# Attention scores in eight array tiles, and layer-norm products in four 64x64 tiles, in a fused ViT tower layer on one core

## The chip, the cores and the metric

One core of one Trainium2 chip (trn2) runs the kernel. The metric is the device time of one execution in microseconds, the median of three runs; the profile shown is of one further execution.

## The reference, cut to what matters

Sixteen images of 64 patches are tokenised (two layer norms, projections, SiLU), and the 64 tokens are repeated three times, with a class token ahead: 193 rows of 64 features per image. Then attention with 8 heads of 8 features, whose weights are a softmax plus a relative bias, a layer norm, a residual, another norm, and a routed feed-forward.

```python
h = tok(x)                                   # [16, 192, 64]; three copies of 64 tokens
h = concat([cls_tok, h], axis=1)             # 193 rows
u = layernorm(h)
attn = softmax(q @ k.T * E**-0.5) + rel_bias # 8 heads; q, k, v from u
h = h + layernorm(attn @ v) * gamma + beta
u = layernorm(h)
w = u @ wr + br                              # top 95 of 193 rows of each image are processed
y = gelu(u @ w1 + b1) @ w2 + b2              # 64 -> 256 -> 64
out = where(chosen, y * w, 0) + u + h
```

## The kernel before, in words

Features lie on partitions. Two images form a pair: image 0 of it on partitions 0 to 63, image 1 on 64 to 127, so that eight pairs (`NP`) stand side by side in the free dimension. `bank[0..7]` are the eight PSUM banks, each a tensor of its own. Every engine has one queue of instructions, in the order written, and semaphores between them; there is no planner, so the order is that of the calls: TensorE's (PE) from L1119 on, ScalarE's (ACT) from L399 and L506, VectorE's (DVE) from L739 and L849, GpSimd's (POOL) from L267.

- **Ahead of attention.** `fold` (L1110) sums the bias table's Toeplitz pieces in banks 6 and 7, and `fold_out` (L732) copies them to `rT`, turned by one column so that the class row comes last, in two copies each. `class_sums` (L1029) and `residual_rows` (L1173, one product of 512 columns into bank 2, taken to `hb` at L489) follow later.
- **Attention** goes in four chunks `c` of two pairs. `scores(c)` (L1193) is eight matmuls of 32 rows by 64 columns of weights and 256 columns streamed, into banks 3 and 4 (`SB`): head group g picks the bank, image i the partitions, pair p the half of the bank. Four different places of the array are used, twice. DVE's `softmax_in(c)` (L815) takes the maxima (two reductions, L819), clips them (L821), and subtracts them (L826, two instructions). The next `scores` waits for the last of these. ACT takes the exponential (`exps`, L455), PE turns it (`turn`, L1212, four transposes into bank 6 or 7, `TB[g]`), ACT copies it out to `eT` (`weights_out`, L470), and PE multiplies with the values (`weigh`, L1225). DVE's `normalise(c)` (L829) divides, `softmax_turn(c)` (L1248, four 64x64 matmuls) turns it back and ACT copies it to `pvT` (L485).
- **The bias part**: `table(t, g)` (L1257) is four matmuls of 128 columns, copied out by ACT (`table_out`, L462), added to by POOL (L309) and turned by `table_turn` (L1273). DVE's `add_parts(g)` (L870) sums the parts into `zz`. The class query has a path of its own: `class_query` on PE (L1185) and DVE (L788), `class_query_sums` and `class_query_end`.
- **The two norms.** For each of four groups g of two pairs: `centre` (L1328; 128x128 weights, 386 columns), `squares` on ACT (L545), `variance` (L1338; 128x128 weights with two blocks of ones), `inverse_stds` on ACT (L550: a logarithm L336 and an exponential L339), and on DVE `residual(g)` (L892: L894, L899 twice, L902), which writes `h2`, for the first norm ("z"), `norm(g)` (L906) for the second ("h"). POOL adds `x2` and `h2` to `xh` (L316).
- **Feed-forward.** `route` (L1403) gives the routing weights, on which DVE runs twelve rounds of "eight largest" (L931, L933) and writes `mw` (L936, L938). `up(m)` and `down(m)` (L1369, L1385) are pairs of matmuls in two array tiles; ACT loads the GELU table (L573) and applies it (L586). When the last `down` is done, PE spreads `mw` (L1444), DVE multiplies, DVE and POOL add `xh`, and SP (SyncE) stores.

## Time and profile before

| | us |
|---|---|
| median of three runs (88.22 to 92.36) | 88.4 |
| the profiled execution, its own time | 88.42 |
| its span, first to last instruction | 86.5 |
| PE busy in it | 78.2 |
| DVE busy | 57.5 |
| ACT busy | 55.8 |
| POOL busy | 18.2 |

The rows further down come from the profiled execution. Its own time is 1.92 us above its span. Matmuls are pipelined: the timeline's duration of one reaches to its modelled end, past the start of the next, so that what a step holds PE for is read from the chain of waits, which shows starts and the time to the next. A 4-byte matmul appears as two records ("x2"), a transpose as one.

### The profile page before, as it was taken

How to read it: one execution, taken by the hardware profiler on the slowest of the kernel's cores; microseconds unless marked ns; L12 is line 12 of the kernel's file. 1: busy time of each engine (PE TensorE's matmuls, PEld its weight loads, DVE VectorE, ACT ScalarE, POOL GpSimd, SP SyncE). 2: the span in 40 equal slices, each digit the busy share in tenths (PEclk: the TensorE clock that was granted, in tenths of full speed). 3: DMA queues.
4: the chain of work that ended last, by engine and by line, in shares of the span. 5: the costliest groups of instructions: out<-in, count | busy, mean ns of one | idle time of the engine just before them, and what ended most of it. 6: DMA issues, size and time to landing. Idle time of an engine off the chain costs nothing.

```text
span 86.5 us, 1796 instructions
## 1 busy us (share of the span) xinstructions
PE 78.2 (90%) x638; PEld 49.8 (58%) x638; DVE 57.5 (66%) x188; ACT 55.8 (65%) x122; POOL 18.2 (21%) x31
## 2 busy tenths in 40 slices
PE   3999999999799999999998998999999799999800
PEld 1585758698478457769787865654523242446500
DVE  0299339439465994979989338389925799993860
ACT  0518247788558389885927272799999968995000
POOL 7000000000024553569150000000086300000620
PEclk9999999999999999999999999999999999999995
DMA  1937991000000000000000000000000000000045
GB/s 28 284 139 240 322 361 39 0 0 4 8 0 0 0 11 0 0 0 0 0 8 0 0 0 8 0 0 0 0 0 0 4 0 0 0 0 8 0 152 213
DMA packets 2568, 3.95 MB, mean 46 GB/s; under 512 B 544, under 2 KB 2048, under 8 KB 2560
## 3 DMA queue, kind: packets, MB, share of 16 engines
q1 hardware_dynamic: 1984, 3.31, 12.0%
q10 hardware_dynamic: 576, 0.53, 1.8%
q8 instruction: 5, 0.08, 0.4%
q14 instruction: 3, 0.02, 0.1%
HBM read 3.05 MB, written 0.79 MB: 44 GB/s over the span
## 4 chain that ended last, share of the span: by engine, by line
PE 78%; ACT 8%; DVE 6%; issue 3%; DVEq 1%; POOL 1%; ACTq 0%; POOLq 0%
PE bank L1398 7%; PE bank L1345 6%; PE bank L1335 6%; PE bank L1380 6%; PE bank L1207 5%; PE bank L1268 5%; PE bank L1222 4%; PE bank L1241 4%; PE bank L968 4%; PE bank L960 3%; PE bank L1444 3%; PE bank L1045 3%; PE bank L1253 2%; PE bank L1081 2%; PE bank L1063 2%
## 5 line engine op out<-in xcount | busy, mean ns | idle before, releaser
L586 ACT ACTIVATE gl<-bank,ffw 128x386 f32<-128x386 f32 x16 | 8.1, 583 | 1.0 <-PE bank L1380 1.0
L316 POOL TENSOR_TENSOR xh<-x,h 128x386 f32<-128x386 f32 x4 | 4.0, 1002 | 18.9 <-DVE x L908 18.9
L474 ACT ACTIVATE eT<-bank 128x512 f32<-128x512 f32 x8 | 4.7, 593 | 4.0 <-PE bank L1241 4.0
L1380 PE MATMUL bank<-x,ffw 64*128 64x386 f32 x32 | 6.8, 522 | 0.5 <-ACT gl L586 0.5
L284 POOL TENSOR_SCALAR xTm<-xT,xclsT 128x256 f32<-128x256 f32 x2 | 1.9, 929 | 24.0 <-DVE xT L728 24.0
L1345 PE MATMUL bank<-zq,same 128*128 128x386 f32 x16 | 6.6, 493 | 0.0
L819 DVE TENSOR_REDUCE mx<-bank 128x8 f32<-128x512 f32 x8 | 5.2, 686 | 2.1 <-PE bank L1207 2.0
L309 POOL TENSOR_TENSOR tb<-tb,cterm 128x512 f32<-128x512 f32 (+1 forms) x4 | 5.1, 1270 | 5.4 <-ACT tb L466 5.4
L1398 PE MATMUL bank<-gl,ffw 128*64 128x386 f32 x32 | 6.1, 500 | 0.0
L1241 PEld LDWEIGHTS bank<-vx,eT 128*64 128x64 f32 x128 | 4.3, 137 | 2.0 <-issue 1.2
L826 DVE TENSOR_TENSOR e_in<-bank,mx 128x512 f32<-128x512 f32 x8 | 5.2, 686 | 0.1
L876 DVE TENSOR_TENSOR zz<-bank,pvT 128x192 f32<-128x192 f32 x8 | 2.5, 353 | 4.1 <-ACT pvT L485 2.7
L1241 PE MATMUL bank<-vx,eT 128*64 128x18 f32 x128 | 4.8, 213 | 0.3 <-ACT eT L474 0.3
L346 ACT ACTIVATE pfm<-bank 96x512 f32<-96x512 f32 x4 | 2.4, 589 | 4.3 <-PE bank L968 4.3
L1114 PE MATMUL bank<-toep,idn 128*128 128x193 f32 x24 | 5.1, 335 | 0.0
L1222 PE MATMUL bank<-idn,e 128*128 128x128 f32 x32 | 5.0, 280 | 0.0
L1380 PEld LDWEIGHTS bank<-x,ffw 64*128 64x128 f32 x32 | 2.6, 185 | 4.0 <-issue 3.7
L459 ACT ACTIVATE e<-e_in 128x512 f32<-128x512 f32 x8 | 4.8, 622 | 0.0
L336 ACT ACTIVATE rstd<-bank,eps 128x386 f32<-128x386 f32 x8 | 4.6, 578 | 0.2
L322 POOL TENSOR_TENSOR zq<-zr,xh 128x386 f32<-128x386 f32 x2 | 2.0, 1030 | 12.9 <-DVE zr L944 12.9
L1268 PEld LDWEIGHTS bank<-vx,rT 128*128 128x128 f32 (+1 forms) x32 | 3.8, 164 | 1.3 <-issue 1.1
L1268 PE MATMUL bank<-vx,rT 128*128 128x128 f32 (+1 forms) x32 | 4.4, 280 | 0.0
(187 smaller groups left out, 183.1 us busy)
## 6 DMA issues: line engine op xcount, KB each, us to landing
out<-zq SPq DMA_DIRECT2D x4, 193.0 KB, 2.1
toep<-toeplitz SPq DMA_DIRECT2D x1, 642.0 KB, 4.1
vx<-vx_start SPq DMA_DIRECT2D x1, 576.0 KB, 6.0
ptm<-patches_tm ACTq DMA_DIRECT2D x2, 192.0 KB, 3.4
ptm<-patches_tm SPq DMA_DIRECT2D x2, 192.0 KB, 3.5
atw<-attw SPq DMA_DIRECT2D x1, 352.0 KB, 2.8
ffw<-ffnw SPq DMA_DIRECT2D x1, 321.0 KB, 6.4
cst<-const SPq DMA_DIRECT2D x1, 131.0 KB, 4.8
```

What stands on the lines that cost most here:

```text
L309: pool.tensor_tensor(tb[0:rows_t, t, 8 * g:8 * g + 8, :], tb[0:rows_t, t, 8 * g:8 * g + 8, :], bc(cterm[0:rows_t, t].rearrange("p h d -> p ...
L586: act.activation(gl[:, 2 * (m % SLOTS) + t, :], bank[UB[m % 2][t]][:, 0:GC], ACT.Gelu_apprx_tanh, bias=b1[:, m % 2:m % 2 + 1]).then_inc(s[ ...
L819: dve.tensor_reduce(mx0[:, c, g, :], sc[g], AX, ALU.max).then_inc(s["mx0_ready"], 1)
L826: dve.tensor_tensor(e_in[:, g], sc[g], bc(mx[:, c, g, :], 2, J), ALU.subtract)\
L1114: last = pe.matmul(bank[6 + b // 2][:, S * (b % 2):S * (b % 2) + S], ident, toep[:, b, J * c:J * c + S], start=(c == 0), stop=(c == 2))
L1222: last = pe.transpose(bank[TB[g]][:, 128 * b:128 * b + 128], e[:, g, 128 * b:128 * b + 128], ident)
L1241: last = pe.matmul(bank[PVB[c]][r, 72 * j + 18 * b:72 * j + 18 * b + 18], eT[:, g, 2 * j + hh, r], vx[:, 2 * c + j, b, 2 * i:2 * i + 2, :] ...
L1268: last = pe.matmul(out_v[:, :, :, b, :].rearrange("q a t c -> q (a t) c"), rT[:, b, 128 * t:128 * t + rows_t], vx[:, 4 * g:4 * g + 4, b, : ...
L1335: pe.matmul(bank[CB[g]][:, 0:GC], cent, src, start=True, stop=True)\
L1345: pe.matmul(bank[RB[g]][:, 0:GC], same_image, zq[:, g, :], start=True, stop=True)\
L1380: last = pe.matmul(bank[UB[m % 2][t]][:, 0:GC], view(ffw, FFNW, "ffn_w1")[r, 128 * c:128 * c + 128], x2[r, g, :], start=True, stop=True)
L1398: last = pe.matmul(bank[FB[g]][64 * t:64 * t + 64, 0:GC], view(ffw, FFNW, "ffn_w2")[:, 64 * c:64 * c + 64], gl[:, 2 * (m % SLOTS) + t, :], ...
```

## The change

Each part, in the order of the kernel:

- The eight PSUM banks become one tensor of eight banks, and banks are dealt anew. `SB` is now a bank for each head group and image (banks 2, 3, 6, 7), and `scores` puts the pair j on the partitions: its eight matmuls stand on eight different places of the array. DVE reads two banks in one instruction. The halves of `eT`, `mx`, `weigh` change index accordingly.
- All turned attention weights go through one bank (`TB = 4`), apart from the last, which uses bank 7; a `turn` waits for the copy-out of the turn before.
- `softmax_turn` is one 128x128 transpose; `table` is two matmuls of 256 columns instead of four of 128.
- `centre` is two 64x64 matmuls, from rows r to the other half of the output partitions; `variance` is two 64x64 matmuls from rows r to the same half. So each `centre` swaps the two images of a pair. `residual_rows` is done in the same swapped way in two halves, earlier, into bank 7. The second `centre` swaps back. Since `xh` needs `h2` unswapped, SP issues eight transfers from `h2` into a new tile `h2_own`, and POOL's additions wait for all eight.
- The class row is first instead of last, so `rT` is copied in one instruction for two, `wts` and `mw` are written by one instruction each, and the host no longer reorders the output.
- The order of calls on PE, ACT and DVE changes around all of these.

```diff
-BT = (5, 3, 4, 2)
-CB = (5, 3, 4, 2)
-RB = (6, 7, 1, 0)
+BT = (5, 3, 6, 2)
+CB = (5, 3, 6, 2)
+RB = (4, 7, 1, 0)
...
-WB = 6
-FB = (4, 0, 2, 6)
+WB = 4
+FB = (6, 0, 2, 4)
...
-KB, QB, VB = (6, 6), (2, 5), (7, 0)
+KB, QB, VB = (4, 4), (2, 5), (1, 0)
...
-SB, TB = (3, 4), (6, 7)
+SB, TB = ((2, 3), (6, 7)), 4
...
+            for g in range(G):
+                sp.wait_ge(s["h2_ready"], 3 * g + 3)
+                for t in range(2):
+                    r, r_other = slice(64 * t, 64 * t + 64), slice(64 - 64 * t, 128 - 64 * t)
+                    sp.dma_start(h2_own[r, g, :], h2[r_other, g].rearrange("p a q -> p (a q)"))\
+                        .then_inc(s["h2_own_ready"], 16)
...
             for g in range(G):
                 pool.wait_ge(s["x2_ready"], g + 1)
-                pool.tensor_tensor(xh[:, g, :], x2[:, g, :], h2[:, g].rearrange("p a q -> p (a q)"),
-                                   ALU.add).then_inc(s["xh_ready"], 1)
+                pool.wait_ge(s["h2_own_ready"], 32 * G)
+                pool.tensor_tensor(xh[:, g, :], x2[:, g, :], h2_own[:, g, :], ALU.add).then_inc(s["xh_ready"], 1)
...
             square4(1)
+            residual_rows_out()
             keys(0)
             head_keys(0, (2, 3))
             std4(1)
             values_out(0)
-            residual_rows_out()
+            keys(1)
+            queries()
+            values_out(1)
             class_key_exp(0)
-            keys(1)
-            values_out(1)
-            queries()
             exps(0, 0)
             exps(0, 1)
+            values_rows_out()
             head_keys(1, (2, 3))
...
             squares("z", 0)
-            softmax_part_out(2)
             squares("z", 1)
+            squares("z", 2)
             softmax_part_out(3)
             inverse_stds("z", 0)
-            squares("z", 2)
             inverse_stds("z", 1)
...
-                dve.tensor_copy(rT[:, 2 * i:2 * i + 2, 0:S - 1], src[:, :, 1:S]).then_inc(s["rT_ready"], 1)
-                dve.tensor_copy(rT[:, 2 * i:2 * i + 2, S - 1:S], src[:, :, 0:1]).then_inc(s["rT_ready"], 1)
+                dve.tensor_copy(rT[:, 2 * i:2 * i + 2, :], src).then_inc(s["rT_ready"], 1)
...
             def softmax_in(c):
-                sc = [bank[SB[g]][:, :].rearrange("p (h k) -> p h k", k=J) for g in range(2)]
+                sc = [banks[:, SB[g][0]:SB[g][0] + 2, 0:256].rearrange("p i (h k) -> p i h k", k=J)
+                      for g in range(2)]
...
             class_query()
             softmax_in(2)
+            normalise(0)
             class_query_sums()
-            normalise(0)
             softmax_in(3)
             normalise(1)
+            normalise(2)
             class_query_end()
...
             add_parts(0)
             add_parts(1)
-            normalise(2)
+            add_parts(2)
             normalise(3)
-            add_parts(2)
             add_parts(3)
...
             def scores(c):
...
-                for p in (2 * c, 2 * c + 1):
+                for j in range(2):
                     for i in range(2):
                         for g in range(2):
                             r = slice(64 * i + 32 * g, 64 * i + 32 * g + 32)
-                            last = pe.matmul(bank[SB[g]][64 * i:64 * i + 64, 256 * (p % 2):256 * (p % 2) + 256],
-                                             qT[r, p, :], k_h[r, p].rearrange("p h k -> p (h k)"),
+                            last = pe.matmul(bank[SB[g][i]][64 * j:64 * j + 64, 0:256], qT[r, 2 * c + j, :],
+                                             k_h[r, 2 * c + j].rearrange("p h k -> p (h k)"),
                                              start=True, stop=True)
...
             def turn(c, g):
                 pe.wait_ge(s["e_ready"], 2 * c + g + 1)
-                if c:
-                    pe.wait_ge(s["eT_ready"], 2 * c + g - 1)
-                elif g == 0:
+                t = bank[TB]
+                if (c, g) == (0, 0):
                     pe.wait_ge(s["kT_ready"], 2)
+                elif (c, g) == (NC - 1, 1):
+                    t = bank[SB[1][1]]
+                    pe.wait_ge(s["ein_ready"], 2 * NC)
                 else:
-                    pe.wait_ge(s["vx_ready"], 1)
-                    pe.wait_ge(s["vx2_ready"], 1)
+                    pe.wait_ge(s["eT_ready"], 2 * c + g)
...
             def softmax_turn(c):
                 pe.wait_ge(s["o_ready"], c + 1)
-                for j in range(2):
-                    for i in range(2):
-                        r = slice(64 * i, 64 * i + 64)
-                        last = pe.matmul(bank[PVB[c]][r, 256 + J * j:256 + J * j + J], o[r, c, J * j:J * j + J],
-                                         ident[r, r], start=True, stop=True)
-                last.then_inc(s["pvT_psum"], 1)
+                pe.transpose(bank[PVB[c]][:, 256:384], o[:, c, :], ident).then_inc(s["pvT_psum"], 1)
...
             scores(0)
-            residual_rows()
             keys(1)
+            queries(1)
             values(1)
-            queries(1)
             values_rows()
             scores(1)
-            table(*TABLE[0])
             turn(0, 0)
             class_query()
+            table(*TABLE[0])
+            turn(0, 1)
+            weigh(0, 0)
+            scores(2)
+            turn(1, 0)
             table(*TABLE[1])
-            turn(0, 1)
-            scores(2)
+            weigh(0, 1)
+            weigh(1, 0)
+            turn(1, 1)
             table(*TABLE[2])
-            turn(1, 0)
-            weigh(0, 0)
-            weigh(0, 1)
-            turn(1, 1)
-            table(*TABLE[3])
             scores(3)
-            weigh(1, 0)
             softmax_turn(0)
             turn(2, 0)
-            table_turn(0)
+            table(*TABLE[3])
             weigh(1, 1)
             turn(2, 1)
             weigh(2, 0)
+            softmax_turn(1)
+            weigh(2, 1)
+            table_turn(0)
             table_turn(1)
             turn(3, 0)
+            softmax_turn(2)
+            turn(3, 1)
             table_turn(2)
-            softmax_turn(1)
-            turn(3, 1)
-            weigh(2, 1)
+            weigh(3, 0)
...
-                pe.matmul(bank[CB[g]][:, 0:GC], cent, src, start=True, stop=True)\
-                    .then_inc(s["zc_psum" if name == "z" else "hc_psum"], 1)
+                for t in range(2):
+                    r, r_other = slice(64 * t, 64 * t + 64), slice(64 - 64 * t, 128 - 64 * t)
+                    last = pe.matmul(bank[CB[g]][r_other, 0:GC], cent[r, r], src[r, :], start=True, stop=True)
+                last.then_inc(s["zc_psum" if name == "z" else "hc_psum"], 1)
...
-                pe.matmul(bank[RB[g]][:, 0:GC], same_image, zq[:, g, :], start=True, stop=True)\
-                    .then_inc(s["zvar_psum" if name == "z" else "hvar_psum"], 1)
+                for t in range(2):
+                    r = slice(64 * t, 64 * t + 64)
+                    last = pe.matmul(bank[RB[g]][r, 0:GC], same[r, r], zq[r, g, :], start=True, stop=True)
+                last.then_inc(s["zvar_psum" if name == "z" else "hvar_psum"], 1)
 
             centre("z", 0)
-            weigh(3, 0)
             weigh(3, 1)
-            softmax_turn(2)
             centre("z", 1)
+            centre("z", 2)
             variance("z", 0)
             softmax_turn(3)
             table_turn(3)
-            centre("z", 2)
             variance("z", 1)
...
             route(0)
             variance("h", 3)
+            up(0)
             route(1)
-            up(0)
             route(2)
...
             down(2)
+            up(6)
             down(3)
-            up(6)
             up(7)
```

## Rows read from the trace of the kernel before

**Rows 1.** The page, busy time by engine: busy us (share), records.

```profile
PE 78.2 (90%) x638; PEld 49.8 (58%) x638; DVE 57.5 (66%) x188; ACT 55.8 (65%) x122; POOL 18.2 (21%) x31
```

**Rows 2.** Table of stretches: length, then busy us of each engine, granted clock, DMA share, GB/s.

```profile
33.60:50.10 16.50, 16.24 (x226) 13.29 (x222) 13.64 (x32) 10.95 (x25) 6.34 (x5) 1.00 0.00 1
...
55.05:66.17 11.12, 11.12 (x42) 5.08 (x40) 7.65 (x22) 10.60 (x23) 2.59 (x3) 1.00 0.00 0
66.17:79.05 12.88, 12.31 (x70) 4.71 (x70) 10.97 (x41) 10.93 (x20) 1.42 (x2) 1.00 0.01 2
```

**Rows 3.** The chain of waits, attention and norms: start, us, engine, tile, line.

```profile
24.70 0.85 PE bank L1036 x8
...
28.00 1.02 PE bank L1207 x16
29.02 1.05 PE bank L1176 x2
...
34.72 0.44 PE bank L1222 x4
...
38.35 1.09 PE bank L1268 x8
...
43.98 0.38 PE bank L1253 x8
...
45.97 0.61 ACT eT L474
...
46.71 0.65 PE bank L1241 x16
...
57.33 0.65 PE bank L1345 x2
```

**Rows 4.** Timeline of DVE, attention stage; in brackets the idle time before it.

```profile
33.70 1.29 DVE L819 TENSOR_REDUCE mx<-bank 128x8 f32<-128x512 f32 x2 [1.33 <-PE bank L1207]
...
35.23 1.29 DVE L826 TENSOR_TENSOR e_in<-bank,mx 128x512 f32<-128x512 f32 x2
...
36.44 0.68 DVE L791 TENSOR_REDUCE cq_m<-bank 128x8 f32<-128x512 f32 x1
...
38.42 1.29 DVE L819 TENSOR_REDUCE mx<-bank 128x8 f32<-128x512 f32 x2 [0.37 <-PE bank L1207]
...
43.47 1.29 DVE L819 TENSOR_REDUCE mx<-bank 128x8 f32<-128x512 f32 x2 [0.26 <-PE bank L1207]
...
51.08 0.62 DVE L876 TENSOR_TENSOR zz<-bank,pvT 128x192 f32<-128x192 f32 x2 [2.48 <-ACT pvT L485]
```

**Rows 5.** Timeline of ACT and DVE in the two norms.

```profile
55.05 0.58 ACT L336 ACTIVATE rstd<-bank,eps 128x386 f32<-128x386 f32 x1
...
60.71 0.62 DVE L894 SCALAR_TENSOR_TENSOR zr<-bank,tkw,rstd 128x386 f32<-128x386 f32 x1
...
60.95 0.58 ACT L336 ACTIVATE rstd<-bank,eps 128x386 f32<-128x386 f32 x1
...
61.91 0.16 DVE L902 TENSOR_TENSOR h<-zr,hb 128x2 f32<-128x2 f32 x1
...
62.37 0.57 ACT L336 ACTIVATE rstd<-bank,eps 128x386 f32<-128x386 f32 x1
```

**Rows 6.** The chain of waits, feed-forward.

```profile
71.88 0.80 PE bank L1398 x4
...
76.48 2.74 PE bank L1398 x16
```

**Rows 7.** DMA issues: KB each, median us from issue to landing.

```profile
out<-zq SPq DMA_DIRECT2D x4, 193.0 KB, 2.1
```

**Rows 8.** Timeline, first and last of the feed-forward: ACT's table, DVE's last routing row.

```profile
66.17 1.28 ACT L573 ACT_TABLE_LOAD   x1
...
78.48 0.15 DVE L938 SCALAR_TENSOR_TENSOR mw<-cur,wts 128x1 f32<-128x1 f32 x1
```

More of the change, by code:

```diff
@@ L94, in sem @@
             return ctx.enter_context(nc.semaphore(name))
-        bank = [ctx.enter_context(nc.psum_tensor(f"bank{i}", [128, 512], F32)) for i in range(8)]
+        banks = ctx.enter_context(nc.psum_tensor("bank", [128, 8, 512], F32))
+        bank = [banks[:, i, :] for i in range(8)]
         ptm = sb("ptm", 128, NT, PF)
@@ L465, in table_out @@
                 act.wait_ge(s["tb_psum"], n + 1)
-                act.activation(tb[0:rows_t, t, 8 * g:8 * g + 8, :],
-                               bank[5][0:rows_t, :].rearrange("p (a f) -> p a f", a=8), ACT.Copy)\
+                act.activation(tb[0:rows_t, t, :, 32 * g:32 * g + 32],
+                               bank[5][0:rows_t, :].rearrange("p (a f) -> p a f", a=B), ACT.Copy)\
                     .then_inc(s["tb0_ready"], 1)
@@ L473, in weights_out @@
                     act.wait_ge(s["pv_psum"], c)
-                act.activation(eT[:, g].rearrange("p a n -> p (a n)"), bank[TB[g]][:, :], ACT.Copy)\
+                t = bank[SB[1][1] if (c, g) == (NC - 1, 1) else TB]
+                act.activation(eT[:, g].rearrange("p a n -> p (a n)"), t[:, :], ACT.Copy)\
                     .then_inc(s["eT_ready"], 1)
@@ L492, in residual_rows_out @@
                 act.wait_ge(s["hbias_ready"], 1)
-                act.activation(hb[:, :, 0:J], bank[2][:, :].rearrange("p (a j) -> p a j", a=NP), ACT.Identity,
+                act.activation(hb[:, :, 0:J], bank[7][:, :].rearrange("p (a j) -> p a j", a=NP), ACT.Identity,
                                bias=hbias[:, :]).then_inc(s["hb_ready"], 1)
@@ L497, in values_rows_out @@
                 act.wait_ge(s["vt_psum"], 1)
-                act.activation(vT[:, :, :], bank[2][:, :].rearrange("p (a j) -> p a j", a=NP), ACT.Copy)\
+                act.activation(vT[:, :, :], bank[1][:, :].rearrange("p (a j) -> p a j", a=NP), ACT.Copy)\
                     .then_inc(s["vT_ready"], 1)
@@ L1027, in class_projections, with class_sums @@
                           view(atw, ATTW, "wv")[0:64, :], start=True, stop=True).then_inc(s["cls_psum"], 1)
-            def class_sums(t):
+            def class_sums(t, bs):
                 n = (128, J + 1)[t]
                 pe.wait_ge(s["cls_qkv"], 3)
-                pe.wait_ge(s["rT_ready"], 4)
+                pe.wait_ge(s["rT_ready"], 2 if 0 in bs else 1)
                 pe.wait_ge(s["in_const"], 16)
-                for b in range(4):
+                for b in bs:
                     last = pe.matmul(bank[1][0:n, 32 + 8 * t + 2 * b:34 + 8 * t + 2 * b], rT[:, b, 128 * t:128 * t + n],
@@ L1108, in queries, with residual_rows @@
                     .then_inc(s["q_psum"], 1)
+            def residual_rows(a):
+                pe.wait_ge(s["h1_ready"], a + 1)
+                pe.wait_ge(s["rT_ready"], 1)
+                for t in range(2):
+                    r, r_other = slice(64 * t, 64 * t + 64), slice(64 - 64 * t, 128 - 64 * t)
+                    last = pe.matmul(bank[7][r_other, 256 * a:256 * a + 256], view(atw, ATTW, "wp2_bd")[r, r],
+                                     h1T[r, 256 * a:256 * a + 256], start=True, stop=True)
+                if a:
+                    last.then_inc(s["hf_psum"], 1)
             def fold(b, cs):
@@ L1152, in _ @@
             fold(1, (0, 1))
+            fold(1, (2,))
             project3(0)
-            fold(1, (2,))
+            class_sums(0, (2, 3))
+            residual_rows(0)
             variance4(0)
+            class_sums(0, (0, 1))
             project3(1)
-            class_sums(0)
+            residual_rows(1)
             keys(0)
-            queries(0)
+            class_sums(1, range(4))
             variance4(1)
@@ L1188, in class_query @@
                 pe.wait_ge(s["kT_ready"], 2)
-                pe.wait_ge(s["vT_ready"], 1)
-                pe.matmul(bank[2][:, :], qcls_m[:, :], kT[:, :], start=True, stop=True)\
+                pe.wait_ge(s["vx_ready"], 2)
+                pe.wait_ge(s["vx2_ready"], 2)
+                pe.matmul(bank[0][:, :], qcls_m[:, :], kT[:, :], start=True, stop=True)\
                     .then_inc(s["cq_psum"], 1)
@@ L1235, in weigh @@
                 pe.wait_ge(s["eT_ready"], 2 * c + g + 1)
-                for j in range(2):
+                for i in range(2):
                     for hh in range(2):
-                        for i in range(2):
-                            r = slice(64 * i, 64 * i + 64)
+                        for j in range(2):
+                            r = slice(64 * j, 64 * j + 64)
                             b = 2 * g + hh
-                            last = pe.matmul(bank[PVB[c]][r, 72 * j + 18 * b:72 * j + 18 * b + 18],
-                                             eT[:, g, 2 * j + hh, r],
+                            last = pe.matmul(bank[PVB[c]][r, 72 * i + 18 * b:72 * i + 18 * b + 18],
+                                             eT[:, g, 2 * i + hh, r],
                                              vx[:, 2 * c + j, b, 2 * i:2 * i + 2, :].rearrange("p t d -> p (t d)"),
@@ L1496, in _lay_out @@
     tc = np.zeros((2, 128, H), np.float32)
-    tc[0] = table[S:S + 128]
-    tc[1, 0:J] = table[S + 128:S + 3 * J]
-    tc[1, J] = table[S - 1]
+    tc[0] = table[S - 1:S + 127]
+    tc[1, 0:J + 1] = table[S + 127:S + 3 * J]
     vx0 = np.zeros((2, 64, NP, 4, 2, 2, D + 1), np.float32)
```

132 lines of the change are left out of this document (64 added, 68 removed).

## The prediction

> **What bounds the kernel now.** I began with busy time by engine: PE is busy for 78.2 of 86.5 us, DVE and ACT for under 58 each [rows 1]. Taken alone this says that PE is the bound and that four array tiles instead of one should pay. The table of stretches says otherwise [rows 2]. In attention (33.6 to 50.1) PE is busy for 16.24 of 16.50 us, but DVE for 13.64 too; in the norms (55.05 to 66.17) PE for all 11.12 and ACT for 10.60. So I read the chain for what each step holds PE for [rows 3], the timeline of DVE for what it waits for [rows 4], and the norms' timeline for a period [rows 5].
>
> In attention there is a loop: `scores(c+1)` waits until DVE has subtracted chunk c, and DVE then waits for `scores(c+1)`. DVE's idle ahead of chunks 1, 2 and 3 is 1.33, 0.37 and 0.26 us, and later it waits 2.48 us for `pvT` of chunk 1 ahead of the second group's sum, because PE turns that chunk late [rows 4]. In the norms everything has one period: logarithm to logarithm on ACT 62.37 - 60.95 = 1.42 us, and DVE's residual from 60.71 to 61.91 + 0.16 = 62.07, 1.36 and a start each 1.4 [rows 5]. PE needs 2 x 0.65 = 1.3 for a centre and a variance [rows 3]. Three engines are tied; relieving PE alone shortens nothing here.
>
> **The parts and their costs.** The sum goes against the profiled execution, 88.42 us, 0.02 above the median, with 1.92 outside the span.
>
> *Ahead of the first scores.* `class_sums` (0.85 for one set of four [rows 3]) and the class column's copies move into idle places; `project3(1)`, the first keys and ACT's logarithm for the second half keep their inputs. The first scores still need the query copy, which DVE now does last. I take 0 for the start at 28.0 and keep -0.1 to +0.4, the upper end being half a `class_sums` that falls on the path.
>
> *Scores.* Before: eight matmuls on four places, two rounds, 1.02 [rows 3]. A round is 256 columns; one `variance` of 386 columns takes 0.65 [rows 3], so a round is 256/386 x 0.65 = 0.43, and 1.02 = 2 x 0.43 + 0.16 for entering the mode. With eight places one round is left: 0.43 + 0.16 = 0.6, unless sixteen records can't be issued so fast; `weigh` issues sixteen in 0.55 to 0.65 [rows 3], so 0.6 stands. Gain 0.4 for each of three chunks on the path. Bounds: 0 (no overlap in one row strip) and 0.5.
> The row that bears on this is `down`: its two matmuls use all 128 rows and different columns, and sixteen records, eight matmuls, take 2.74, 0.34 each, half of 0.65 [rows 3, 6]. So neighbours in one row strip do overlap.
> The Trainium skill, "TensorE: Matmul & The Clock Gate", Part 3, "The mechanism", says that a weight load overlaps running matmuls only when its row group differs; by that the new scores and norm tiles would gain nothing (the second rival). The trace's `down` disagrees with it.
>
> *The schedule of attention.* I redid it with the rows' durations: PE to DVE 0.15 us, PE to ACT 0.3, ACT to PE 0.13 (46.58 to 46.71 [rows 3]); ACT's 512-element operations 0.55 to 0.6; `softmax_in` 2 x 1.29 + 0.2 = 2.8 (33.70 to 36.44 [rows 4]); the class query on DVE 1.6. `residual_rows` (1.05 [rows 3]) no longer stands between the first scores and the second keys, and `table(0)` (1.09) no longer between scores and turn.
> Chunk 0 leaves DVE at 31.75, scores(1) is issued at once instead of behind `values_rows`, and DVE starts chunk 1 at 32.5 instead of 33.70. It ends it at 35.25, does the class query to 36.85 and finds scores(2) (issued 35.8, done 36.5) ready: chunk 2 at 36.85 instead of 38.42, to 39.65. Then normalise(0) and the class sums, 1.75, to 41.4; scores(3) is ready by 40.9; chunk 3 at 41.4 instead of 43.47, to 44.2. So 2.1 us are gained there, and DVE is the bound: behind chunk 3 come normalise(1), a wait of 1.0 for `weigh(2, 1)`, normalise(2), the end of the class query and three sums, to 49.75. PE centres group 0 at 48.55, then weighs the last half chunk, centres groups 1 and 2, and multiplies variance 0 beside centre 2, done at 51.3. The 2.48 us wait is gone; late instead is ACT's queue, which holds the squares of groups 0 to 2 and the last `pvT`: its first logarithm is at 52.2 instead of 55.05 [rows 5]. Gain 2.85.
> `softmax_turn` falls from 0.38 to the 0.11 of one transpose (four take 0.44 [rows 3]), `table` from 1.09 by the three starts saved to some 0.9; both are inside this schedule.
> An unknown is DVE's reading over two banks. The shortest rows of one bank cost 1.29/2 for 512 elements, 1.26 ns each; the cut-up sums of L876 0.31 for 192, 1.61 ns each [rows 4]. At the latter rate each of sixteen instructions costs 0.18 more, 2.9 together. I take 0, as the new pattern still runs 64 elements in a row and the cut into heads is there already.
>
> *The norms.* Centre and variance now lie side by side, 0.65 to 0.8 a pair for 1.3. ACT doesn't get shorter: eight logarithm-exponential pairs and the squares, 11.12 us from 55.05 [rows 2, 5]. One square (group 2), 0.4, is now done ahead, so from 52.2 it lasts 10.7, to 62.9 instead of 66.17. That is 3.25 gained, all but 0.4 of it from attention. The tiles' own share here is nothing: PE gets idle. What they would be worth on top is bounded by 0 and by 8 x 0.65 = 5.2, and the ACT row puts it at the low end; without it the swap of halves would not be needed.
>
> *The transfers* stand on SP's queue, which holds only the output's behind them. A transfer of 193 KB takes 2.1 us [rows 7]; those of 99 KB for the last group start near 59 and land near 62. POOL's four additions (1 us each) end by 67 at the latest. Nobody needs `xh` until `mw` is ready, 78.6 [rows 8]. Cost 0; without that cover a late one would cost its 2 us once.
>
> *Feed-forward.* It hangs on ACT's last exponential (the table load starts at 66.17 [rows 8], and GELU after it) and on the routing that follows the last `x2`. DVE's routing becomes shorter by two single-column instructions, 0.15 and 0.2, but PE is later than `mw`: its `down` block, 76.48 + 2.74, ends after 78.63 [rows 6, 8]. The new order splits down 2, down 3, up 6, up 7 into four blocks for two. A `down` alone takes 0.80, in a block 2.74/4 = 0.69 [rows 6]: 0.11 a block, with `up` somewhat more, so I take +0.3 (0 to +0.4).
>
> Sum: 88.42 - 3.25 + 0.3 = 85.5. A hand-made schedule has each instruction start the moment that its input is there. For what slips (a copy-out behind another, seven turns through one bank) I add 0.4, an estimate from the idle times of 0.26 and 0.37 that the present kernel shows in a like place [rows 4]. **Forecast 85.9 us.**
>
> **Rivals.**
> 1. *The turning bank becomes the bound* (slower). With one bank for seven of eight turns, a turn can't start until ACT has copied the last one out: 0.3 + 0.61 + 0.13 = 1.04 us [rows 3], and this copy stands in ACT's queue behind exponentials, head keys and table copies. In my schedule scores, tables and `weigh` cover it, but it already makes the second turn of chunk 0 one to two us later than its exponential. For it: ACT is busy for 10.95 of 16.5 in attention [rows 2] and its order is fixed. Against it: DVE is the busier one. Each round trip that isn't covered costs 1.04; from the third on, 85.9 + 2.5 is reached and the change is a loss. With four, 90.1; I price it at 89.8.
> 2. *No overlap within a row strip.* Scores stay at 1.02, 3 x 0.4 = 1.2 back, and the norm's pairs at 1.3 plus entering the mode, about 0.4: 87.5. Against it: `down`.
> 3. *DVE pays for two banks*: 85.9 + 2.9 = 88.8, as DVE is the bound.
> 4. *PE's clock falls.* The granted clock is 1.00 in all the stretches [rows 2], with PE never short of work. In the norms it would now be busy for about half of the time. If the level falls from 2.4 to 1.2 GHz there, a side-by-side pair takes 1.3, still inside ACT's 1.42, but the first blocks of the feed-forward would run at half speed: four of them at 0.8 more each, about 89. The Trainium skill, the page named above, Part 1, says that activity releases the throttle; no run here shows what half a load does.
> 5. *Better than scheduled*: no slip, and no cost of the split blocks: 84.8.
>
> **How the numbers follow.** Forecast 0.50 (its own range 85.2 to 87.0); rival 1 0.12, rival 2 0.12, rival 3 0.08, rival 4 0.06, rival 5 0.12. The range 84.6 to 88.8 leaves out about 0.05 below and 0.12 above. Two per cent, about what a measurement of this kernel can tell from no change, is 1.77 us. Under 86.6: 0.44 of the forecast, rival 5, and 0.05 of rivals 2 and 3, 0.61. Over 90.2: half of rival 1 and of rival 4, 0.10 with what isn't named. Between: 0.29.
>
> **What would show it.** Right: a `scores` step of about 0.6 in the chain, DVE's first maxima of chunks 1 to 3 near 32.5, 36.9 and 41.4, the wait of 2.48 gone, ACT's first norm logarithm near 52.2 and a period of 1.42 from there, the table load near 62.9, PE idle by a third or more in the norms, and from there to the end the same length or 0.3 more. Wrong: idle DVE in attention with PE waiting for `eT`; a reduction over 0.7 us; a granted clock under 1 behind the norms; a period in the norms well under 1.42, which would mean that ACT wasn't bound; POOL's additions reaching past the end of the routing.

## The result, and the profile after

The kernel after takes 86.26 us (median of four runs, 86.0 to 90.86) against 88.32 us (median of four, 88.22 to 92.36) for the kernel before beside it. The ratio is 0.9761, 95% interval 0.9728 to 0.9794: 2.1 us less (1.8 to 2.4). Forecast were 85.9 us, with a range of 84.6 to 88.8. The profiled execution took 86.00 us, its span is 84.2.

One thing must be known before any two traces are laid side by side: the first products of an execution run at half rate for a time that differs from execution to execution, with the same code. The first `variance2` product started at 12.2 us in this trace, at 13.0 in the trace before, and between 12.4 and 15.8 in those below, most of which leave the code ahead of it alone. Executions that were over 1.5% slower than the fastest of their kernel, as those that began late are, stay out of the ratios. I read every trace from that product on, in four stretches, each ending at an instruction's start: the first `scores` (start), the first logarithm of the norms (attention), the GELU table load (norms), the end of DVE's last addition (feed-forward).

| stretch, us | before | after | measured | forecast |
|---|---|---|---|---|
| start: first `variance2` to first `scores` | 14.97 | 15.32 | +0.35 | 0 |
| attention: to the first logarithm | 27.12 | 25.26 | -1.86 | -2.85 |
| norms: to the table load | 11.12 | 10.46 | -0.66 | -0.4 |
| feed-forward: to DVE's last addition | 17.42 | 17.88 | +0.46 | +0.3 |
| slips | | | | +0.4 |
| sum | 70.63 | 68.92 | -1.71 | -2.55 |

The profiled executions differ by 88.42 - 86.00 = 2.42: the 1.71, plus 0.74 from the earlier first product, less 0.03 behind DVE's last addition. The 0.74 lies within what one and the same code shows from execution to execution, so I don't count it as the change's. The nearly right total thus hides a gain that was forecast 0.8 us too high.

Busy time by engine, kernel after (answers to [rows 1]):

```profile
PE 72.9 (87%) x632; PEld 43.9 (52%) x632; DVE 57.7 (69%) x184; ACT 55.6 (66%) x122; POOL 18.1 (21%) x31
```

PE lost 5.3 us of work and the kernel 2 us: the other engines' work is as it was.

Table of stretches, kernel after: attention, norms, feed-forward to the spreading of `mw` (columns as in [rows 2]):

```profile
32.50:50.00 17.50, 15.80 (x211) 11.58 (x209) 15.56 (x40) 11.96 (x28) 6.25 (x5) 1.00 0.00 1
...
52.80:63.26 10.46, 8.82 (x65) 2.71 (x64) 7.46 (x22) 10.16 (x23) 1.02 (x2) 1.00 0.32 76
63.26:76.63 13.37, 12.29 (x68) 4.41 (x66) 10.79 (x39) 10.81 (x20) 2.86 (x3) 1.00 0.01 2
```

In attention DVE, busy for 15.56 of 17.50, has all but caught up with PE, 15.80. In the norms PE idles for 1.6 us, ACT hardly at all, and the clock stays at 1.00.

The chain of waits, kernel after (start, us, what; answers to [rows 3] and [rows 6]):

```profile
31.44 0.62 PE bank L1227 x16
...
37.45 0.60 PE bank L1263 x16
...
38.13 0.61 ACT eT L483
...
38.88 0.65 PE bank L1263 x16
...
43.19 0.60 PE bank L1263 x16
...
43.87 0.61 ACT eT L483
...
44.61 0.63 PE bank L1243 x4
...
70.62 0.80 PE bank L1416 x4
71.42 0.07 issue
71.49 0.92 PE bank L1398 x4
72.41 0.80 PE bank L1416 x4
73.21 0.85 PE bank L1398 x4
```

`scores` (L1227) holds PE for 0.62 instead of 1.02. At two places PE runs dry for 0.83, from 38.05 to 38.88 and from 43.79 to 44.61: ACT's copy to `eT` (L483) begins only when a `weigh` (L1263) has ended, because `eT` has one buffer and `weights_out(c, g)` waits until all of chunk c-1 is weighed. The kernel before has the same wait in its code, and its chain shows it once for 0.83, with the rows 45.97 and 46.71 of [rows 3]. New is the one at 38.05, which lies ahead of `scores(3)`.

DVE's timeline, attention stage, kernel after (answers to [rows 4]):

```profile
32.16 1.29 DVE L828 TENSOR_REDUCE mx<-bank 128x8 f32<-128x512 f32 x2 [0.40 <-PE bank L1227]
33.48 0.17 DVE L830 TENSOR_SCALAR mx<-mx 128x16 f32<-128x16 f32 x1
...
36.43 1.28 DVE L828 TENSOR_REDUCE mx<-bank 128x8 f32<-128x512 f32 x2
...
40.56 0.71 DVE L811 SCALAR_TENSOR_TENSOR cq_den<-cq_c,cq_s 128x8 f32<-128x8 f32 x1
...
41.73 1.29 DVE L828 TENSOR_REDUCE mx<-bank 128x8 f32<-128x512 f32 x2 [0.23 <-PE bank L1227]
43.06 0.60 DVE L830 TENSOR_SCALAR mx<-mx 128x16 f32<-128x16 f32 x1
...
46.70 0.17 DVE L844 SCALAR_TENSOR_TENSOR den<-ec,bank 128x16 f32<-128x16 f32 x1 [1.02 <-PE bank L1263]
```

POOL's timeline, the same stretch:

```profile
39.90 1.26 POOL L317 TENSOR_TENSOR tb<-tb,cterm 65x512 f32<-65x512 f32 x1 [2.47 <-ACT tb L474]
41.13 1.28 POOL L314 TENSOR_TENSOR cq_v<-cq_e,vT 128x512 f32<-128x512 f32 x1
42.37 1.26 POOL L317 TENSOR_TENSOR tb<-tb,cterm 128x512 f32<-128x512 f32 x1
```

The wait of 2.48 is gone, and two reductions, each over two banks, cost 1.29, as over one. But two tiny operations are stretched: the clip of the maxima (L830) takes 0.17 or 0.60, and `cq_den`, 128x8 elements, 0.71. Both long ones end within 0.11 us of the end of a POOL operation (39.90 + 1.26 = 41.16, 42.37 + 1.26 = 43.63). The Trainium skill, "SBUF — State Buffer", "Who interferes with whom", gives the reason: VectorE and GpSimd share one pair of SBUF ports as an exclusive lock, which an operation with two SBUF inputs or in a two-port mode needs and `tensor_reduce` never does. By that rule, the trace agrees: the large reductions beside the same POOL operations keep their 0.64, and so do subtractions, which have one input in PSUM (1.29 for two from 40.22 in the trace before, beside a POOL operation from 40.15).

ACT's timeline, kernel after (answers to [rows 5]):

```profile
52.80 0.59 ACT L344 ACTIVATE rstd<-bank,eps 128x386 f32<-128x386 f32 x1
...
56.80 0.58 ACT L344 ACTIVATE rstd<-bank,eps 128x386 f32<-128x386 f32 x1
...
58.21 0.58 ACT L344 ACTIVATE rstd<-bank,eps 128x386 f32<-128x386 f32 x1
...
63.26 1.28 ACT L582 ACT_TABLE_LOAD   x1
```

The period is 58.21 - 56.80 = 1.41, as before.

### The profile page after: what moved, and what is told of

The parts are those of the page before. It is cut to its first block, busy times and chain, and to the rows that moved or that the text cites. A ratio compares the mean times of both kernels' runs of the same rounds, so it can differ in the third digit from the quotient of the medians.

```text
span 84.2 us, 1799 instructions
## 1 busy us (share of the span) xinstructions
PE 72.9 (87%) x632; PEld 43.9 (52%) x632; DVE 57.7 (69%) x184; ACT 55.6 (66%) x122; POOL 18.1 (21%) x31
## 4 chain that ended last, share of the span: by engine, by line
PE 72%; ACT 16%; DVE 4%; issue 3%; DVEq 1%; POOL 1%; ACTq 0%; POOLq 0%
PE bank L1416 7%; PE bank L1398 6%; PE bank L1263 6%; PE bank L1131 5%; PE bank L1243 5%; PE bank L1285 4%; ACT rstd L347 4%; ACT rstd L344 3%; PE bank L974 3%; PE bank L1353 3%; PE bank L966 3%; PE bank L1462 3%; ACT zq L557 3%; PE bank L1227 2%; PE bank L1051 2%
## 5 line engine op out<-in xcount | busy, mean ns | idle before, releaser
L325 POOL TENSOR_TENSOR xh<-x,h_own 128x386 f32<-128x386 f32 x4 | 3.9, 1003 | 16.0 <-DMA h_own<-h 16.0
L483 ACT ACTIVATE eT<-bank 128x512 f32<-128x512 f32 x8 | 4.7, 592 | 3.9 <-PE bank L1263 3.1
L1365 PE MATMUL bank<-zq,same 64*64 64x386 f32 x32 | 6.9, 508 | 0.1
L1263 PE MATMUL bank<-vx,eT 128*64 128x18 f32 x128 | 5.2, 213 | 0.8 <-ACT eT L483 0.8
L1263 PEld LDWEIGHTS bank<-vx,eT 128*64 128x64 f32 x128 | 4.4, 137 | 2.9 <-issue 2.6
L557 ACT ACTIVATE zq<-bank 128x386 f32<-128x386 f32 x8 | 3.9, 483 | 2.1 <-PE bank L1353 2.1
L1353 PE MATMUL bank<-h,cst 64*64 64x386 f32 x16 | 3.5, 510 | 1.5 <-DVE h L912 1.3
L330 POOL TENSOR_TENSOR zq<-zr,xh 128x386 f32<-128x386 f32 x2 | 2.0, 1012 | 12.2 <-DVE zr L950 12.2
L1243 PEld LDWEIGHTS bank<-idn,e 128*128 128x128 f32 x32 | 3.5, 141 | 1.8 <-issue 1.3
```

Source lines behind the costliest of these rows:

```text
L557: act.activation(zq[:, g, :], bank[CB[g]][:, 0:GC], ACT.Square)\
L1243: last = pe.transpose(t[:, 128 * b:128 * b + 128], e[:, g, 128 * b:128 * b + 128], ident)
L1263: last = pe.matmul(bank[PVB[c]][r, 72 * i + 18 * b:72 * i + 18 * b + 18], eT[:, g, 2 * i + hh, r], vx[:, 2 * c + j, b, 2 * i:2 * i + 2, :] ...
L1353: last = pe.matmul(bank[CB[g]][r_other, 0:GC], cent[r, r], src[r, :], start=True, stop=True)
L1365: last = pe.matmul(bank[RB[g]][r, 0:GC], same[r, r], zq[r, g, :], start=True, stop=True)
```

## The experiments

Four groups, each on one chip beside runs of the kernel before. All are edits of the kernel after. Stretches as above, in us; the ratio is to the kernel before.

| run | start | attention | norms | feed-forward | sum | ratio, 95% |
|---|---|---|---|---|---|---|
| before | 14.97 | 27.12 | 11.12 | 17.42 | 70.63 | 1 |
| after | 15.32 | 25.26 | 10.46 | 17.88 | 68.92 | 0.9761 [0.9728, 0.9794] |
| c0_changed | 15.32 | 25.27 | 10.45 | 17.90 | 68.94 | 0.9808 [0.9715, 0.99] |
| e1_ff_order | 15.32 | 25.27 | 10.45 | 17.41 | 68.45 | 0.9787 [0.9724, 0.985] |
| e2_full_norms | 15.10 | 25.74 | 10.92 | 17.90 | 69.66 | 0.99 [0.981, 0.9989] |
| e3_two_eT | 16.63 | 28.52 | 10.44 | 17.90 | 73.49 | 1.0204 [1.0153, 1.0254] |
| e4_two_eT_order | 15.31 | 29.44 | 10.45 | 17.89 | 73.09 | none |
| e5_third_round | 15.32 | 28.51 | 10.45 | 17.89 | 72.17 | 1.0176 [1.009, 1.0262] |
| e6_all | 15.31 | 29.24 | 10.45 | 17.41 | 72.41 | 1.0263 [1.0203, 1.0323] |
| e7_residual_later | 15.72 | 25.26 | 10.46 | 17.91 | 69.35 | 0.9871 [0.9812, 0.993] |
| e8_no_shared_port | 15.31 | 25.37 | 10.45 | 17.88 | 69.01 | 0.9837 [0.9796, 0.9878] |
| e9_all_no_shared_port | 15.32 | 23.35 | 10.45 | 17.39 | 66.51 | 0.9514 [0.9487, 0.9542] |
| e10_dry_spell_filled | 15.31 | 24.98 | 10.45 | 17.39 | 68.13 | 0.9697 [0.964, 0.9754] |
| e11_best_third_round | 15.31 | 24.82 | 10.46 | 17.40 | 67.99 | 0.9728 [0.9687, 0.977] |

The stretches repeat to 0.03 us in every run that doesn't touch them (e3's start apart), so they tell apart what a ratio can't, whose interval reaches 0.25 to 0.8 us to either side. By their ratios alone most of these runs can't be told from the kernel after; what they price is read from the stretches of one trace each.

**c0_changed.** The kernel after, unedited.

> The changed kernel itself, as the measure for the others of this group: 86.2 us by every theory, first norm logarithm at 52.8 and table load near 63.3 in its trace. A second profile also tells how much of the 0.39 us by which its first scores started earlier than before (27.54 against 27.93) comes back: if the lead stays it is a part of the gain, if it goes it was the arrival of the input.

Every stretch came back; the first `variance2` product stood at 14.74 instead of 12.22, which is 2.5 of the 2.8 us by which this execution, at 88.81, was longer. The chain of waits of c0_changed, early:

```profile
7.84 1.05 PE bank L1051 x4
...
9.84 1.05 PE bank L1051 x4
10.89 0.85 PE bank L1062 x8
```

The same three steps take 0.58, 0.58 and 0.44 in the trace of the kernel after.

**e1_ff_order.** The calls of the feed-forward in the old order.

```diff
+            down(3)
             up(6)
-            down(3)
```

> The feed-forward's old order of blocks (down 2, down 3, up 6, up 7). Theory: splitting them costs two changes of array mode, so 0.3 to 0.5 us come back, about 85.8, and the stretch from the table load to the spreading of mw goes from 13.5 back to 13.1. Rival: the routing on DVE or ACT's GELU bounds that stretch, then no change, 86.2.

0.49 us came back. Chain of waits of e1_ff_order at the same place:

```profile
70.15 0.85 PE bank L1398 x4
71.00 1.45 PE bank L1416 x8
72.45 1.50 PE bank L1398 x8
```

Two `down` in one block take 1.45 against 2 x 0.80, two `up` 1.50 against 0.92 + 0.85, and 0.07 of waiting goes: 0.15 + 0.27 + 0.07 = 0.49. The break between kinds of tile costs more where it ends at an `up`.

**e2_full_norms.** Centres, variances and residual rows as 128x128 products again, with no swap and no transfers.

```diff
-                for t in range(2):
...
-                    last = pe.matmul(bank[CB[g]][r_other, 0:GC], cent[r, r], src[r, :], start=True, stop=True)
...
+                pe.matmul(bank[CB[g]][:, 0:GC], cent, src, start=True, stop=True)\
...
-                    last = pe.matmul(bank[RB[g]][r, 0:GC], same[r, r], zq[r, g, :], start=True, stop=True)
...
+                pe.matmul(bank[RB[g]][:, 0:GC], same_image, zq[:, g, :], start=True, stop=True)\
...
```

> Centres and variances as 128x128 products again, residual rows unswapped, no transfers of h2; all else as changed. Theory: ACT bounds the norms with its period of 1.41 us, so PE's 64x64 tiles buy nothing by themselves: 86.2, within 0.3, the period of the logarithms still 1.41 to 1.44. Rival: side-by-side tiles carry a good part of the gain: 87.0 or more, with PE as the releaser of ACT's squares and a period of 1.5 or over. A second rival, that the eight transfers cost something by sharing memory with the engines: faster, under 86.0.

The tiles are worth 0.48 ahead of the first logarithm and 0.46 behind it, and their residual rows cost 0.22 at the start: 0.72 net. ACT's timeline of e2_full_norms shows where:

```profile
57.55 0.58 ACT L338 ACTIVATE rstd<-bank,eps 128x386 f32<-128x386 f32 x1 [0.16 <-PE bank L1353]
...
58.97 0.57 ACT L338 ACTIVATE rstd<-bank,eps 128x386 f32<-128x386 f32 x1
```

In the middle the period is 58.97 - 57.55 = 1.42, so ACT is the bound with either kind of tile. The tiles pay at the joints. Ahead of the first logarithm PE makes two centres and a variance, side by side in 1.46 us (50.77 to 52.23 in the chain of the kernel after) and one behind the other in 2.14 here (50.81 to 52.95). Behind it, of the seven intervals from logarithm to logarithm, the second, the third and the last are 0.14, 0.15 and 0.17 longer here; at the passage from the first norm to the second (57.55) and at the end (63.03) ACT waits for a variance. The transfers cost nothing behind the table load, where the stretches with and without them are equal (17.88 and 17.90); in the norms this run takes away the transfers and the tiles together and can't tell them apart. So the theory, no change, and the rival's period of 1.5 were both wrong.

**e3_two_eT.** A second buffer of `eT`, so that a copy-out waits for the chunk before the last.

```diff
...
-                if c:
-                    act.wait_ge(s["pv_psum"], c)
+                if c > 1:
+                    act.wait_ge(s["pv_psum"], c - 1)
...
-                                             eT[:, g, 2 * i + hh, r],
+                                             eT[:, c % 2, g, 2 * i + hh, r],
```

> A second buffer for the turned weights eT, so that a copy-out no longer waits for the last chunk's products; PE's two waits of 0.83 us (38.05 and 43.79 in the changed kernel's trace) go. Theory: DVE is the bound in attention and gets back only its 0.23 us ahead of chunk 3; from the first scores to the first norm logarithm 25.26 falls to about 25.0, 86.0 in all. Rival: PE's waits were on the path, 2 x 0.83: 23.6, about 84.6.

The waits for `eT` went, and the kernel became 2% slower than the one before. The start stretch was 1.3 longer in this execution, and the half rate accounts for it, not the edit (e4, e6 and e9 have the same buffers and 15.3): here it reached past the first `variance2`, and the first five steps of PE's chain from there took 3.30 us against 2.02 in the kernel after. Attention took 3.3 more, and the granted clock was 0.50 from 51 to 57 us. What lowered it shows better in e6.

**e4_two_eT_order**, the same with `weigh(2, 1)` ahead of `softmax_turn(1)`, and **e6_all**, e4 with e1's order and ACT's `exps(3, 0)` ahead of `softmax_part_out(1)`.

```diff
+            weigh(2, 1)
             softmax_turn(1)
-            weigh(2, 1)
```

> As e3_two_eT, and PE weighs the second half of chunk 2 ahead of softmax_turn(1) instead of behind it, so that DVE's normalise(2) needn't wait the 1.02 us. Theory (DVE bound): 1.0 less than e3_two_eT from first scores to first norm logarithm, about 24.1, 85.0 in all. Rival: ACT's queue (exponentials of chunk 3 behind the copy of pvT) is next and holds it at 24.7 or more.

> As e4_two_eT_order, with the feed-forward's old order of blocks, and ACT taking the first exponential of chunk 3 ahead of the copy of pvT. By the theories: 0.49 less than e4_two_eT_order behind the table load (13.37 to 12.88, which e1_ff_order showed), and 0.2 to 0.4 less ahead of the norms: 84.3. If ACT isn't next, only the 0.49: 84.5.

Both came out far above that. Table of stretches of e6_all:

```profile
44.00:48.00 4.00, 2.45 (x38) 2.24 (x39) 3.79 (x11) 1.94 (x5) 0.78 (x1) 0.74 0.00 0
48.00:51.00 3.00, 3.00 (x17) 2.91 (x16) 1.55 (x8) 1.35 (x4) 0.00 (x0) 0.50 0.00 0
...
54.00:57.00 3.00, 3.00 (x26) 1.52 (x25) 0.71 (x3) 0.78 (x3) 0.00 (x0) 0.64 0.00 0
```

The granted clock falls from 2.4 to 1.2 GHz near 46 us, inside a stretch in which PE was busy for 2.45 of 4.00, and stays there for most of the time to 56. PE had just idled from 44.54 to 45.59, waiting for `eT`. In e4 five of six executions had a mean clock of 0.93 and took 90.44 us or more; the sixth, of the same code, had 0.987 and took 86.36, which leaves no ratio. Why PE ran dry stands in DVE's timeline of e6_all:

```profile
41.24 1.59 DVE L811 SCALAR_TENSOR_TENSOR cq_den<-cq_c,cq_s 128x8 f32<-128x8 f32 x1
...
44.25 0.55 DVE L830 TENSOR_SCALAR mx<-mx 128x16 f32<-128x16 f32 x1
```

and in POOL's:

```profile
40.31 1.27 POOL L314 TENSOR_TENSOR cq_v<-cq_e,vT 128x512 f32<-128x512 f32 x1
41.55 1.26 POOL L317 TENSOR_TENSOR tb<-tb,cterm 128x512 f32<-128x512 f32 x1
```

With PE no longer held, the table reaches POOL 1.5 us earlier, counted from the first `scores`, and `cq_den` meets another pair of its operations: it is held through the rest of one and all of the next, until 41.55 + 1.26 = 42.81. In the kernel after POOL's operations follow each other as closely, and there `cq_den` got its turn between two of them, at 41.16; what decides which it will be no run shows. Chunk 3 leaves DVE late. ACT's queue has the exponential of its maxima ahead of the copy of `eT` for chunk 2, so that ACT idles for 1.40 us, and PE, which needs the copy, for 1.05.

**e5_third_round.** `scores` issues its first four products twice (the result is the same), so that the step costs PE what it did before.

```diff
-                for j in range(2):
+                for j in (0, 0, 1):
```

> Each chunk of scores issues its first four products twice, so that a chunk takes two rounds on PE as before the change (about 1.05 us instead of 0.62). Theory: the one-round scores gain their 0.43 us on each chunk that DVE waits for, and DVE waits for chunks 1 and 3 (idle 0.40 and 0.23) but is late itself at chunk 2: 0.43 + 0.43 lost of 1.3, about 87.1. Rival: PE's order decides everything there, then all three count, 87.5 or more. Rival: DVE has slack enough, then 86.3.

The step went from 0.62 to 1.02, and attention from 25.26 to 28.51. Four rounds of 0.4 are 1.6; the rest I put down to the clock, which fell again. Table of stretches of e5_third_round:

```profile
48.00:51.30 3.30, 2.45 (x46) 2.03 (x44) 1.78 (x7) 2.61 (x7) 1.26 (x1) 1.00 0.00 0
51.30:54.80 3.50, 3.50 (x24) 3.27 (x24) 2.57 (x11) 1.84 (x4) 0.00 (x0) 0.52 0.02 5
```

So this run can't price the round; e11 was made for that. Its PE waits twice for 0.85 us, hardly more than the twice 0.83 of the kernel after, whose clock held: what decides whether it falls stays open.

**e7_residual_later.** `residual_rows(0)` behind `variance4(0)`.

```diff
+            variance4(0)
             residual_rows(0)
-            variance4(0)
```

> residual_rows(0), the 64x64 products ahead of variance4(0), moved behind it. Theory: they cost 0.22 us before the first scores (from variance2(0) to the first scores 15.32 us, 15.10 with 128x128 products in e2_full_norms, 14.97 before the change); 15.1 here and 86.05 in all. Rival: not their place but the later queries set it: 15.3, 86.26.

It got worse by 0.40 at the start, against both theory and rival: PE now idles for 0.32 ahead of `variance4(0)`, where these products used to be, and the second half's next product, `project3(1)`, starts 0.55 later. So of the 0.35 lost at the start, 0.22 is known from e2 as the price of doing these rows in tiles; the other 0.13 stays open.

**e8_no_shared_port.** `cq_den` and the two clips become reductions, which don't need POOL's ports. ACT writes `exp(-m)/3` as a 65th column of `cq_e`, and the maxima get a column of zeros beside them.

```diff
...
-                dve.scalar_tensor_tensor(cq_den[:, :], cq_c[:, :], 1.0 / 3.0, cq_s[:, :], ALU.mult, ALU.add)\
...
+                dve.tensor_reduce(cq_den[:, :], cq_e[:, :, :], AX, ALU.add).then_inc(s["cq_den_ready"], 1)
...
-                    dve.tensor_scalar(mx[:, c], mx0[:, c], 0.0, None, ALU.max)
+                    dve.tensor_reduce(mx[:, c], mx0[:, c], AX, ALU.max)
```

> The changed kernel with DVE's small operations on the softmax replaced: the class denominator's addition (0.71 us in the changed kernel's trace, 0.17 where POOL is idle) is folded into a reduction over one more column that ACT writes, and the clipping of the maxima (0.60 us once, else 0.17) is a reduction over the value and a zero. Theory: these two waited for POOL's running additions, and reductions don't; both go. Chunk 3 is also held by PE (scores(3) issued at 40.94), so of 0.97 us only the 0.43 of the clipping reach the norms: from first scores to first norm logarithm 24.85, about 85.85. Rival: the length is the instructions' own, and a reduction over POOL's running time is as long: no change, 86.26. Second rival: PE then waits longer for its input and its clock falls as in e3_two_eT: 88 or more.

No gain. DVE's timeline of e8_no_shared_port:

```profile
43.03 0.20 DVE L819 RECIPROCAL cq_r<-cq_den 128x8 f32<-128x8 f32 x1
44.27 1.29 DVE L833 TENSOR_REDUCE mx<-bank 128x8 f32<-128x512 f32 x2 [1.04 <-PE bank L1233]
```

DVE is free earlier and then idles for 1.04 until the scores of chunk 3 come, which stand behind PE's wait for `eT`; what the clip gives back goes into a longer wait for `weigh(2, 1)`, 1.44 for 1.02. The two holds lie side by side: to take this one away alone gives nothing.

**e9_all_no_shared_port.** e6 and e8 together.

> e6_all with the same replacement. Theory: in e6_all the class denominator's addition took 1.59 us behind two operations of POOL, so that chunk 3 began 2.4 us after its scores were issued; PE ran dry from 44.4 and its clock fell to half until 56. With the addition gone chunk 3 begins 1.5 us earlier; if the clock holds, from first scores to first norm logarithm about 22.5 us and 83.0 in all. Rival: PE, which has less to do than DVE here, runs dry all the same and the clock falls: 88 or more, logarithm over 27.

DVE's timeline of e9_all_no_shared_port at the same place:

```profile
42.54 0.68 DVE L817 TENSOR_REDUCE cq_den<-cq_e 128x8 f32<-128x520 f32 x1
43.26 0.20 DVE L819 RECIPROCAL cq_r<-cq_den 128x8 f32<-128x8 f32 x1
43.38 1.25 DVE L833 TENSOR_REDUCE mx<-bank 128x8 f32<-128x512 f32 x2
44.66 0.19 DVE L836 TENSOR_REDUCE mx<-mx 128x16 f32<-128x32 f32 x1
```

Nothing is stretched, DVE waits for nothing here, and the clock is 1.00 in every stretch from 44 to 60. Attention takes 23.35, 1.91 less than after the change, though 0.85 more than I expected. When DVE begins to subtract chunk 3 the lead is 1.47, and that much is the two holds', as the calls that e4 and e6 moved come later; the rest, with the wait for `weigh(2, 1)` down from 1.02 to 0.48, may be the new order's, and no run separates it. In the chain of e9_all_no_shared_port a copy through the one turning bank now shows, for which PE waits 0.68:

```profile
45.99 0.60 ACT eT L488
...
46.65 0.65 PE bank L1269 x16
```

At 0.9514, with 83.8 us in the shortest of seven executions (median 86.19), it beats both kernels.

**e10_dry_spell_filled.** e6 with five products of 512 bf16 columns, written where nobody reads, in the place in which PE ran dry (the edit is shown against e6; the trace has a record of four of the five).

```diff
+            pe.wait_ge(s["tb0_ready"], 4)
+            keep_busy(5, 5)
             weigh(2, 1)
```

> e6_all with five idle products (128x128 bfloat16 weights, 512 columns, into a bank that nobody reads) where PE ran dry at 44.4; nothing else. They leave the arithmetic as it is. Theory: the clock fell because PE had too little to do there; with the products it stays at full level, and from first scores to first norm logarithm 29.24 falls to about 24.9 (e9_all_no_shared_port's 23.35 and the 1.6 us by which POOL holds DVE ahead of chunk 3), 85.3 in all. Rival: the fall has another cause, then the length stays over 28, 90.2.

PE's timeline, and below it the table of stretches, of e10_dry_spell_filled:

```profile
43.64 0.65 PE L1263 MATMUL bank<-vx,eT 128*64 128x18 f32 x16
44.44 1.03 PE L966 MATMUL bank<-warm 128*128 128x512 bf16 x4 [0.16 <-issue]
```

```profile
44.00:48.00 4.00, 3.28 (x44) 2.53 (x44) 3.72 (x11) 2.13 (x5) 0.51 (x1) 1.00 0.00 0
```

The clock is 1.00 in the stretches behind, too. One microsecond of products that nobody needs gives back 29.24 - 24.98 = 4.26 us, as expected. That the dry spell brings the clock down in e6 is thereby shown. The run also shows what the second `eT` buffer gives with the clock held and `cq_den` still at 1.59: 0.28, new order included.

**e11_best_third_round.** e9 with e5's edit.

> e9_all_no_shared_port with each chunk's first four scores products issued twice, so that a chunk takes two rounds, as before the change. It measures the price of the second round where the clock has held (in e5_third_round it fell). Theory: DVE waits for chunks 0 and 1 only and starts chunks 2 and 3 straight from other work, so 0.3 + 0.42 are lost: 23.35 from first scores to first norm logarithm becomes 23.9 to 24.1 (the scores' own start is the same), about 84.6. Rival: all four count, 1.7: 25.0, 85.6. Second rival: the clock falls: over 26.

The clock held, and attention took 24.82 - 23.35 = 1.47 more: most of 4 x 0.4. My schedule had put three steps on the path, with DVE's slack behind one of them; nearly all four count (the rival's 25.0 was the better forecast).

## Why the prediction was right, and where it wasn't

- **Scores: right.** A step of 0.6 was forecast, 0.62 came. Eight places run side by side although they share row strips, as `down` had said; the second rival falls. The rule quoted beside it is about weight loads, and these overlapped too: in the `down` block before, from 76.48 to 79.22, the loads (PEld) of the same 128 rows, all but the first four, lie inside the time of its products. The stage's gain from the shorter step is larger than three steps of 0.4, 1.47 measured on e9; on the kernel after itself it has no price, as the clock fell in e5.
- **Reading over two banks: right.** 0.64 a reduction, as before; the third rival falls.
- **Start: wrong by 0.35**, inside its bound of +0.4: "I take 0" should have counted the residual rows, which moved ahead of the second keys, as two tiles more, 0.22 (e2).
- **The schedule of attention: wrong by 1.0**, with 0.4 set aside for it, and by 1.5 with norm products of 128x128 (e2: 25.74 against 24.27). The failed steps are two. "scores(3) is ready by 40.9": I took `weigh` to be ready when its exponential was and left out that `eT` has one buffer, so that PE waits 0.83 ahead of `scores(3)` and once more behind it, though [rows 3] shows such a wait. And "normalise(0) and the class sums, 1.75": these were costed at undisturbed durations, where POOL adds 0.5 to `cq_den`. The trace before had the sign: its clip at 39.74 takes 0.45, beside a POOL operation from 38.89 to 40.16. Measured from the first `variance2`, chunk 1 was 0.4 later than scheduled, chunk 2 0.3, and chunk 3 1.1.
- **Tiles in the norms: wrong.** "The tiles' own share here is nothing" was read from a period, and the period is indeed ACT's. But a stage has joints too, where ACT waits for a product, and two centres and a variance lie ahead of the period altogether. Gross 0.94, net 0.72 (e2), which is over a third of the change's 1.71. In attention 0.48 of it hides half a microsecond of the schedule's error. Two signs named for "right" failed with it: a pair side by side takes 0.97 (53.70 to 54.67), not 0.65 to 0.8, and PE idles for 1.64 of 10.46 in the norms, not for a third. The square done ahead, forecast at 0.4, gave 0.20 (11.12 before, 10.92 in e2); the tiles made up for it.
- **Transfers: right.** `xh` was written from 62.2 to 66.1, 12 us ahead of its use.
- **Feed-forward: sign right, size low**, +0.49 (e1) for +0.3: 0.15 of it at the `down`, 0.27 at the `up`, 0.07 of waiting. The prediction had 0.11 a block, from a quarter of a block of four; a block of two, 1.45, stood in the trace before.
- **First rival, the turning bank:** round trips were uncovered, but by another cause. There are two, of 0.83 instead of 1.04, one more than before; I had put the loss at the third. Their cause is the single `eT`, not the bank: e9 keeps the one bank, and neither of the two is left in its chain. The bank itself shows there once, with 0.68.
- **Fourth rival, the clock:** it stayed at 1.00 in attention, norms and feed-forward. But e3 to e6 show it one step away, and not in the norms, where I looked for it, but in attention. I had put its price at about 3 us; it was 4.26 in e6.

Adding up what was priced: scores -1.5 and norm tiles -0.9, against +0.35 at the start and +0.49 in the feed-forward, give -1.6 of -1.71. So the new order of calls in attention and the cheaper `table` and `softmax_turn` seem to leave next to nothing: what they free goes into the two holds, without which attention is 1.5 to 1.9 shorter (e9). This balance mixes prices from two versions and is argued, not measured as a whole.

## What to carry to other kernels

Before an engine's queue is scheduled by hand, write down each buffer's number of copies and each pair of engines that hold one another, since two holds side by side can hide each other until both are removed. Don't price a stage by its period alone: its first and last turns follow other engines than its middle. And when a faster order leaves TensorE dry, look at the granted clock first: here dummy products were worth four times their time.

## What the runs showed of the hardware

- An operation of DVE on 128x8 elements took 0.17 (before), 0.71 (after) or 1.59 us (e6) by where POOL stood. Between two POOL operations that followed each other it got its turn in the kernel after and didn't in e6.
- TensorE's level fell to 1.2 GHz after PE had idled for 1.05 us (e6), in a stretch busy for 2.45 of 4.00, and held when products filled the place (e10, 3.28 of 4.00) and in the norms of the kernel after (8.82 of 10.46). The same code kept it in one of six executions (e4).
- At the start of an execution products ran at half rate, 1.05 for 0.58 (c0_changed), with a granted clock printed as 1.00 from 7 to 15 us: there the durations tell, not the record. In e3 this reached into the start stretch and cost it 1.3 us.
- Products on eight 32x64 places that share row strips in pairs took 0.62 us (after), the same work on four places 1.02 (before).
